# Another order of first loads and first ScalarE work, and dummy products on TensorE, in a graph-attention and expert kernel

## The reference, cut to what matters

```python
def gat_layer(x, adj, W, a_self, a_neigh, b):
    feat = jnp.einsum('nf,hfo->hno', x, W)
    attn_self = jnp.einsum('hno,ho->hn', feat, a_self)
    attn_neigh = jnp.einsum('hno,ho->hn', feat, a_neigh)
    e = jax.nn.leaky_relu(attn_self[:, :, None] + attn_neigh[:, None, :], 0.2)
    e = e + MASK_VAL * (1.0 - adj)[None, :, :]
    alpha = jax.nn.softmax(e, axis=-1)
    out = jnp.einsum('hnm,hmo->hno', alpha, feat) + b[:, None, :]
    return jax.nn.elu(jnp.transpose(out, (1, 0, 2)).reshape(out.shape[1], -1))
x = x + tanh(g_xattn) * gat_twice(ctx_512, layernorm(x))
x = x + tanh(g_ffn) * (routed_experts(layernorm(x)) + shared_experts(layernorm(x)))
```

## Time and profile before

| | us |
|---|---|
| median of three runs | 427.19 |
| the three runs | 427.02, 427.19, 428.5 |
| the profiled execution | 426.62 |
| its span in the trace | 424.9 |

### The profile page before, as it was taken

How to read it: one execution, slowest core, us unless ns; L and a number is a source line. 1 busy time by engine, 2 the same in 40 slices (tenths; PEclk the granted TensorE clock), 3 DMA queues, 4 the chain that set the end, 5 groups by cost and what they waited for, 6 DMA issues and landing times.

```text
span 424.9 us, 7970 instructions
## 1 busy us (share of the span) xinstructions
PE 379.1 (89%) x2706; PEld 327.9 (77%) x2707; DVE 251.3 (59%) x860; ACT 224.1 (53%) x535; POOL 92.5 (22%) x102
## 2 busy tenths in 40 slices
PE   5986776976999699997998999999999999999991
PEld 4754555654788577885887889999999999999980
DVE  1898979889998946876573423334333334344330
ACT  4699799598866618420210237554646454555410
POOL 6642400000000040132207200312121222212121
PEclk9999697599999979999999999999999999999996
DMA  6149387515050001010899920122222222221221
GB/s 177 41 174 427 145 321 313 201 77 200 2 200 2 0 27 52 2 40 13 323 425 424 380 79 26 25 39 40 48 37 42 37 38 37 39 39 26 25 25 13
DMA packets 17138, 48.68 MB, mean 115 GB/s; under 512 B 3232, under 2 KB 13392, under 8 KB 14160
## 3 DMA queue, kind: packets, MB, share of 16 engines
q1 hardware_dynamic: 11200, 40.80, 25.3%
q0 software_dynamic: 4464, 6.26, 8.4%
q10 hardware_dynamic: 1440, 1.18, 0.8%
HBM read 39.46 MB, written 8.77 MB: 114 GB/s over the span
## 4 chain that ended last, share of the span: by engine, by line
PE 67%; DVE 15%; ACT 11%; issue 2%; POOL 1%; DMA 1%; ACTq 0%; POOLq 0%; DVEq 0%
PE ps_c L797 19%; PE ps_o L815 12%; PE ps_c L644 7%; ACT weights L902 6%; PE ps_n L797 5%; PE ps_pt L651 4%; PE ps_n L644 3%; ACT weights L908 3%; DVE weights L1096 3%; PE ps_pt L563 3%; PE ps_f L552 2%; DVE weights L1107 2%; PE ps_n L651 2%; PE ps_o L578 2%; PE ps_n L516 2%
## 5 line engine op out<-in xcount | busy, mean ns | idle before, releaser
L797 PE MATMUL ps_c<-tile_t,weights 128*128 128x128 f32 x736 | 89.6, 275 | 0.0
L797 PEld LDWEIGHTS ps_c<-tile_t,weights 128*128 128x128 f32 x736 | 87.6, 192 | 1.2
L1157 DVE SCALAR_TENSOR_TENSOR gate_silu<-gate_tanh,ps_c 128x256 f32<-128x256 f32 x76 | 31.9, 420 | 78.2 <-ACT gate_tanh L1001 67.3
L476 POOL DMA_INDIRECT out<-y_sb,tile_in x23 | 35.8, 1555 | 145.5 <-DVE y_sb L1337 145.5
L902 ACT ACTIVATE weights<-weights 128x256 f32<-128x256 f32 x128 | 63.1, 498 | 0.6 <-DVE y_sb L1172 0.6
L1096 DVE SCALAR_TENSOR_TENSOR weights<-weights 128x256 f32<-128x256 f32 x128 | 54.4, 487 | 6.2 <-ACT weights L889 5.8
L1006 ACT ACTIVATE weights<-weights 128x2560 f32 x23 | 53.8, 2337 | 6.1 <-issue 6.1
L644 PE MATMUL ps_c<-x_norm_t,weights 128*128 128x256 f32 x240 | 56.6, 383 | 0.0
L563 PE MATMUL ps_pt<-ident,weights 128*128 128x128 f32 x256 | 39.4, 304 | 18.5 <-ACT weights L908 18.5
L815 PE MATMUL ps_o<-weights,hidden 128*128 x230 | 53.5, 380 | 0.6 <-DVE hidden L1160 0.6
L563 PEld LDWEIGHTS ps_pt<-ident,weights 128*128 128x128 f32 x256 | 32.8, 157 | 26.2 <-issue 25.3
(11 more groups left out here) (207 smaller groups left out, 507.7 us busy)
## 6 DMA issues: line engine op xcount, KB each, us to landing
weights<-w_routed SPq DMA_DIRECT2D x8, 1920.0 KB, 21.0
weights<-t_rows SPq DMA_DIRECT2D x14, 1024.0 KB, 5.7
weights<-w_shared SPq DMA_DIRECT2D x1, 3840.0 KB, 16.2
tile_in<-slots SPq DMA_DIRECT2D x23, 132.0 KB, 2.1
slots<-pad_row SPq DMA_DIRECT2D x1, 1188.0 KB, 11.3
out<-y_sb ACTq DMA_DIRECT2D x4, 256.0 KB, 7.2
weights<-x SPq DMA_DIRECT2D x2, 256.0 KB, 3.7
x_in<-x SPq DMA_DIRECT2D x2, 256.0 KB, 4.2
```

Source lines behind the costliest of these rows:

```text
L476: pool.indirect_dma_start(out=out, out_offset=bass.IndirectOffsetOnAxis(ap=tile_in[:, slot, ID_COL:ID_COL + 1].bitcast(U32), axis=0), in_= ...
L797: mm = pe.matmul(ps_chunk[c][:, part * cw + i * P:part * cw + (i + 1) * P], ring[r % RING][:, a:a + P], tile_t[:, r % 2, k, :], start=(k = ...
```

## The change

SyncE's queue loads the context of graph 0 first, and the attention columns `a_cols` move to ScalarE's queue, behind `w0_t`. VectorE clears `x_norm_t[0]` at the start. TensorE multiplies parts of this cleared tile into `ps_c` 8 times ahead of all else, and 3 times at the end of each of the units 0, 1 and 2; nothing reads these products. The mask of graph 0 is made on VectorE. The bends of units 0 and 1 (the first half of the rows of the first graph) read t from PSUM; those of units 2 and 3 read the copy in SBUF. ScalarE makes the 0.2 t copy first and the t copy after the bends that read PSUM. `mask_stats(1)` stands behind `copy_features(1)`, and the tanh of the gates stands in unit 0.

```diff
@@ -56,6 +56,8 @@
 PEELED = 4
 ROUTED_LOOPS = (SLOT_TILES - WEIGHTS_AHEAD - PEELED) // SLOTS_IN
 QUADS = HEADS // QUAD
+WARM_FIRST = 8
+WARM_STEPS, WARM_EACH = 3, 3
 
 
 
@@ -240,7 +242,8 @@
         ring_filled = sem("ring_filled")
         const_step, ident_ready = sem("const_step"), sem("ident_ready")
         ramp_ready = sem("ramp_ready")
-        wide_ready, wide_copied = sem("wide_ready"), sem("wide_copied")
+        wide_ready, wide_copied, wide_scaled = sem("wide_ready"), sem("wide_copied"), sem("wide_scaled")
+        warm_ready, first_masked = sem("warm_ready"), sem("first_masked")
         nodes_ready, t_copied, s_copied = sem("nodes_ready"), sem("t_copied"), sem("s_copied")
         st_t = sem("st_t")
         ld_t = [[sem(f"ld_t{c}{quad}") for quad in range(QUADS)] for c in range(PAIR)]
@@ -312,7 +315,7 @@
             def load_x(n):
                 sp.dma_start(x_in[n], x[n * N:(n + 1) * N, :].rearrange("(h p) d -> p h d", p=P)).then_inc(ld_x[n], 16)
 
-            sp.dma_start(a_sb, a_cols.rearrange("(c p) a -> p c a", p=P)).then_inc(ld_a, 16)
+            load_ctx(0)
             load_x(0)
             load_ctx(1)
             load_x(1)
@@ -445,12 +448,13 @@
                 for half in range(HV):
                     pool.tensor_scalar(mask[n][:, half, :], x_in[n][:, half, :], stats[c][:, half, 6:7], stats[c][:, half, 7:8],
                                        ALU.subtract, ALU.mult).then_inc(mask_step, 1)
-                pool.wait_ge(mask_step, HV * (n + 1))
+                pool.wait_ge(mask_step, HV * n)
                 pool.tensor_scalar(mask[n], mask[n], 1.0, MASK, ALU.subtract, ALU.mult).then_inc(mask_ready, 1)
 
             for n in range(B):
                 power(n, n % PAIR)
-                make_mask(n, n % PAIR)
+                if n > 0:
+                    make_mask(n, n % PAIR)
             for n in range(B):
                 if n == 2:
                     send_rows(0)
@@ -685,6 +689,13 @@
                     pe.wait_ge(hid_ready, PIECES * n + IC * (e + 1))
                     down(n, half, e, ps_n[:, half * D:(half + 1) * D])
 
+            def keep_warm(count):
+
+                for _ in range(count):
+                    pe.matmul(ps_c[:, 0, 0:P], x_norm_t[0][:, 0, 0:P], x_norm_t[0][:, 1, 0:P], start=True, stop=True)
+
+            pe.wait_ge(warm_ready, 1)
+            keep_warm(WARM_FIRST)
             pe.wait_ge(ident_ready, 1)
             pe.wait_ge(ld_a, 16)
             pe.wait_ge(ld_w0_t, 16)
@@ -727,6 +738,8 @@
                     filler(slots_now[1])
                 if u == 3:
                     spread_inverse(L)
+                if w < WARM_STEPS:
+                    keep_warm(WARM_EACH)
                 if w in TURN_X_NORM:
                     pe.wait_ge(h1_read, TURN_X_NORM[w] + 1)
                     turn_x_norm(TURN_X_NORM[w])
@@ -848,10 +861,11 @@
         @block.scalar
         def _(act):
             act.dma_start(w0_t_sb, w0_t.rearrange("(k p) n -> p k n", p=P)).then_inc(ld_w0_t, 16)
-            act.dma_start(ctx_sb[0][0:F_IN, :], ctx_t[0]).then_inc(ld_ctx[0], 16)
-
-            act.wait_ge(ld_gates, 16)
-            act.activation(tanh_gates, gates_sb, ACT.Tanh).then_inc(gates_ready, 1)
+            act.dma_start(a_sb, a_cols.rearrange("(c p) a -> p c a", p=P)).then_inc(ld_a, 16)
+
+            def make_gates():
+                act.wait_ge(ld_gates, 16)
+                act.activation(tanh_gates, gates_sb, ACT.Tanh).then_inc(gates_ready, 1)
 
             def copy_features(L):
                 act.wait_ge(feat_ready, L + 1)
@@ -864,7 +878,8 @@
                 c = n % PAIR
                 act.wait_ge(ld_x[n], 16)
                 if n >= PAIR:
-                    act.wait_ge(mask_ready, n - PAIR + 1)
+                    act.wait_ge(squares_ready, n - 1)
+                    act.wait_ge(*((mask_ready, n - PAIR) if n > PAIR else (first_masked, 1)))
                 for half in range(HV):
                     act.activation(hidden[:, half * D:(half + 1) * D], x_in[n][:, half, :], ACT.Copy,
                                    accum_out=stats[c][:, half, 4:5]).then_inc(moment_step, 1)
@@ -878,9 +893,12 @@
                 ins.then_inc(squares_ready, 1)
 
             def copy_first_wide(quad):
+                act.wait_ge(bent_ready, quad + 1)
+                act.activation(t_wide[0][:, KINDS * quad, :], ps_wide[quad], ACT.Copy).then_inc(wide_copied, 1)
+
+            def scale_first_wide(quad):
                 act.wait_ge(wide_ready, quad + 1)
-                act.activation(t_wide[0][:, KINDS * quad, :], ps_wide[quad], ACT.Copy)
-                act.activation(t_wide[0][:, KINDS * quad + 1, :], ps_wide[quad], ACT.Copy, scale=LEAK).then_inc(wide_copied, 1)
+                act.activation(t_wide[0][:, KINDS * quad + 1, :], ps_wide[quad], ACT.Copy, scale=LEAK).then_inc(wide_scaled, 1)
 
             def copy_nodes(L):
                 act.wait_ge(nodes_ready, L + 1)
@@ -938,14 +956,16 @@
                 act.wait_ge(y_saved, n + 1)
                 act.dma_start(out[n * N:(n + 1) * N, :].rearrange("(h p) d -> p h d", p=P), y_sb).then_inc(st_base, 16)
 
-            mask_stats(1)
+            scale_first_wide(0)
+            copy_nodes(0)
+            scale_first_wide(1)
             copy_first_wide(0)
-            copy_nodes(0)
-            copy_first_wide(1)
             copy_nodes(1)
             copy_features(0)
             exponent(0)
+            copy_first_wide(1)
             copy_features(1)
+            mask_stats(1)
             for w in range(ALL_UNITS):
                 L, u = w // UNITS, w % UNITS
                 slots_now = filler_slots(w)
@@ -965,6 +985,7 @@
                 if w in NODES_AT:
                     copy_nodes(NODES_AT[w])
                 if w == 0:
+                    make_gates()
                     mask_stats(2)
                 if w == UNITS:
                     mask_stats(3)
@@ -1078,6 +1099,16 @@
                 dve.wait_ge(ld_x[0], 16)
                 row_stats(x_in[0], 0, 1)
 
+            def first_mask():
+
+                dve.wait_ge(inv_ready, 1)
+                for half in range(HV):
+                    ins = dve.tensor_scalar(mask[0][:, half, :], x_in[0][:, half, :], stats[0][:, half, 6:7], stats[0][:, half, 7:8],
+                                            ALU.subtract, ALU.mult)
+                link(ins)
+                dve.tensor_scalar(mask[0], mask[0], 1.0, MASK, ALU.subtract, ALU.mult).then_inc(first_masked, 1)
+                dve.wait_ge(first_masked, 1)
+
             def mask_max(w):
 
                 L, u = w // UNITS, w % UNITS
@@ -1088,18 +1119,21 @@
                 if u == 0:
                     dve.wait_ge(s_copied, L + 1)
                 if L == 0:
-                    dve.wait_ge(wide_copied, quad + 1)
+                    dve.wait_ge(wide_scaled, quad + 1)
+                    if half > 0:
+                        dve.wait_ge(wide_copied, quad + 1)
                 else:
                     dve.wait_ge(ld_t[c][quad], 16 * ((L + 1) // PAIR if c else L // PAIR))
+                neigh = ps_wide[quad] if L == 0 and half == 0 else t_wide[c][:, KINDS * quad, :]
                 for i in range(QUAD):
                     h = quad * QUAD + i
                     ins = dve.scalar_tensor_tensor(out=logits[:, w % AHEAD, i * N:(i + 1) * N],
-                                                   in0=t_wide[c][:, KINDS * quad, i * N:(i + 1) * N],
+                                                   in0=neigh[:, i * N:(i + 1) * N],
                                                    scalar=s_cols[c][:, half, h:h + 1],
                                                    in1=t_wide[c][:, KINDS * quad + 1, i * N:(i + 1) * N], op0=ALU.add, op1=ALU.max)
                 ins.then_inc(bent_ready, 1)
-                if u == 0 and layer == 0:
-                    dve.wait_ge(mask_ready, n + 1)
+                if u == 0 and layer == 0 and n > 0:
+                    dve.wait_ge(mask_ready, n)
                 dve.wait_ge(bent_ready, w + 1)
                 for i in range(QUAD):
                     v = logits[:, w % AHEAD, i * N:(i + 1) * N]
@@ -1256,8 +1290,10 @@
             def tail_piece(n, i):
                 shared_piece(n, i, piece_bank(n, i))
 
+            dve.memset(x_norm_t[0], 0.0).then_inc(warm_ready, 1)
             weigh_columns(0)
             first_mask_stats()
+            first_mask()
             mask_max(0)
             mask_max(1)
             weigh_columns(1)
```

## The result

| | kernel before | changed kernel |
|---|---|---|
| median of seven runs | 428.40 us | 431.41 us |
| all runs | 427.02 to 431.32 | 429.61 to 437.17 |
| profiled execution | 426.62 | 432.18 |
| its span | 424.9 | 430.4 |

The ratio is 1.0074, with a 95% interval of 1.004 to 1.0108: slower by 3.2 us, 1.7 to 4.6. More runs of the kernel before have raised its own median from 427.19 to 428.40, so the change cost 3.0 us between medians, where +3.6 was forecast.

A forecast was written before the change was run, and what follows sets the result against it. TensorE until 20.58 us, then ScalarE's chain of exponents, was taken to bound the kernel. 0.85 + 2.27 + 0.15 + 0.3 = +3.6 us on a median of 427.19 gave 430.8 us, range 424.6 to 431.9.

The forecast's parts named there:

- What bounds the start: TensorE's work until 20.58 us bounds the start, then ScalarE's exponents from unit 1 on, which carry the whole kernel.
- The dummies ahead: Eight products before the column sums on TensorE delay the first wide product from 5.10 to 5.95: +0.85 us at low clock.
- The order of loads: At the start, context earlier and columns second on their queue; both wait for TensorE, so nothing is paid back.
- the clock staying low: TensorE stays at its low clock through the start despite the burst; 430.8 us, chance 0.50.
- the rise with a fall: Rival at the start: TensorE's clock rises in the dummies and falls again in 64-row products; 428.1 us, chance 0.25.
- the rise that holds: Rival at the start: TensorE's clock rises and holds to the end of the features; 424.6 us, chance 0.19.
- The statistics: mask_stats(1) on ScalarE, now between the features' copy and the exponents of unit 1, is no longer hidden: +2.27 us.
- The gates: The gates' tanh comes into ScalarE's busy stretch in unit 0: +0.15 us.
- The dummies of the units: TensorE, units 0 to 2: hidden at high clock, 0.75 us stick out at low clock; booked +0.3 us.
- The mask of graph 1: GpSimd ends it at 31.0 us; VectorE waits 3 us for it, covered with 3.5 us to spare.
- Bends from PSUM: VectorE's bends that read PSUM cost the same as those from SBUF, 1.67 us for four.
- That the shift is carried in full: The whole kernel loses what the exponents of unit 1 lose; rival, not carried: about 427 us, chance 0.06.

The follow-up runs named there:

- run 8: Kernel before with only the cleared tile and the 8 dummies ahead added; 1.0010 of the kernel before.
- run 1: Changed kernel without any dummies and without the clearing of the tile; 1.0067 of the kernel before.
- run 12: Changed kernel measured again, unaltered, in six runs; median 428.14 us against 424.66 of the kernel before on the same chip.
- run 2: Changed kernel with the 8 dummies ahead but none in units 0 to 2; 1.0023 of the kernel before.
- run 4: Changed kernel without any dummies and with mask_stats(1) moved back ahead of the first wide copies; 1.0036 of the kernel before.
- run 10: Changed kernel without unit dummies, mask_stats(1) moved back, layer 1 column sums and second features behind unit 0's transposes; 1.0000 of the kernel before.
- run 11: Changed kernel without dummies, old load order, mask_stats(1) moved back, layer 1 column sums and second features behind unit 0's transposes; 1.0002 of the kernel before.
- run 5: Changed kernel without dummies, mask_stats(1) moved back, and the old order of the two first loads; 0.9985 of the kernel before.
- run 9: Kernel before with only the first units reordered, layer 1 column sums and second features behind unit 0's transposes; 0.9987 of the kernel before.
- run 3: Changed kernel, all dummies kept, with mask_stats(1) moved back ahead of the first wide copies; 1.0000 of the kernel before.

## Why the prediction was right, point by point

**What bounds the start.** Right. TensorE's low-clock products bound the start, and ScalarE from the exponents of unit 1 on. In run 8 TensorE ends the features at 19.39 and the exponents of unit 1 start at 19.92; before it was 20.58 and 21.11, the same half microsecond.

**The dummies ahead.** Right in kind, short in size: +0.85 was booked, +1.2 measured. The clearing began at 0.95, not 0.78, and the records took 0.24 us, the dearer of my two rows. The sum as written had a slip too: 4.9 + 0.58 + 0.04 + 0.3 is 5.82, and I wrote 5.95.

**The order of loads.** Missed. I said both loads would wait for TensorE, which holds with the dummies. I gave no price for the columns behind `w0_t`, and without the dummies that is 0.2 to 1.7 us. It also means that in the changed kernel the burst costs less than it seems, because it covers a late load. This is what run 1 stumbled over.

**The clock.** I gave the case that came in the trace, the clock staying low, 0.50, the rise with a fall 0.25, the rise that holds 0.19. Two traces of six with the 8 dummies show the rise and fall, four the low clock; the runs' mean clock speaks for two in three. The rise that holds came in none of the four traces with an early rise: in each the clock fell among the 64-row products, with TensorE busy. That the 64 rows are the cause isn't isolated by any run. The rival's mechanism was right, its chance too low by half, and the reason that I had for the low clock (zeros, of which no row tells) is not one, since zeros raised it in three traces. The plain rule of the Trainium skill, "TensorE: Matmul & The Clock Gate" (Part 1, "What's actually happening"), that activity releases the throttle, agrees with the long bursts (two of two) and with two of six short ones, not with the products from 5.10 to 20.58. My reading of these was too simple in one point: from 16.69 to 18.51 the column sums of layer 1 stand among them, with 128 rows. The Trainium skill's same page (Part 4, "PE-mode transpose") says that transpose-mode work doesn't count as busy for the clock in the same way. Here the clock rose behind eight transposes at 29.36 and the products next to them, so these records at least didn't keep it down; whether they are of the page's mode no row tells.

**The statistics.** Right: 2.27 forecast, 22.28 to 24.54 = 2.26 measured, and moving them back is the largest part of the loss in the times as well (1.0074 to 1.0000 with the dummies, 1.0067 to 1.0036 without; between medians from 3.0 us to 0.3, and from 3.6 to 1.9).

**The gates.** 0.15 forecast, 0.1 measured (24.54 to 29.77 is 5.23, and 21.11 to 26.25 was 5.14).

**The dummies of the units.** A term that the clock decides: +0.3 was booked, and 0.75 for a low clock. In the profiled execution the low clock lasted. The chain that ended last, of the changed kernel (start, us, engine, what), runs through them:

```profile
34.10 1.71 PE ps_pt L567 x8
...
36.82 0.96 PE ps_c L695 x6
...
39.86 0.60 ACT weights L932
```

The transposes of unit 2 stand behind 1.58 us of dummies, and the copy is 0.9 us later for it. From the exponents of unit 1 to the copy of `ps_f` behind unit 3 (L932 at 39.86) ScalarE takes 15.32 us here. It took 14.10 before (21.11 to 35.21). Run 1 has no dummies and as long a low clock: 14.77. Run 12 has all the dummies and the clock up by 31 us: 14.17. So of the 1.22 us more, 0.1 are the gates, some 0.55 the dummies, and the other 0.6 come with the low clock alone, which in the trace of before had ended by the transposes of unit 3 and here lasted through them in run 1 and until about 36.9 us in the changed kernel. The sum had no term for that. Where the clock is up the dummies are hidden, as was forecast.

**The mask of graph 1.** Right: done at 31.2 (31.0 forecast), a wait of 3.05 us (3), covered by ScalarE's lag. **Bends from PSUM.** Right: 1.66 us for four. The page of the Trainium skill that I had weighed, "Perfetto Trace Analysis" ("Optimizing Scalar/DVE Operations"), would have had them longer by 0.26 us, my estimate from its figures; the trace shows no such difference.

**The sum.** For the low clock the exponents of unit 1 were forecast at 24.2 and start at 24.54 in both traces of the changed kernel. At the end 430.8 was forecast and 431.41 measured, and that is closer than the sum deserves. The kernel before's own median moved up by 1.2 us, and the change cost 3.0 and not 3.6. Up to the copy behind unit 3 the profiled execution lost 4.65 us, 1.05 more than the sum (0.35 in the burst, the rest in the units), and about two executions in three seem to get some 2 us back by a clock that I had at one in four. These errors cancel.

**That the shift is carried in full.** I named as a sign of being wrong that the shift isn't that of the end, and between the two single traces it isn't: 4.65 us at the copy of `ps_f` behind unit 3, nothing at 175 us, 5.5 at the end. Over all the kernels it is carried, though not to the microsecond. The table has that copy in each trace against the 35.21 of before, and the difference of the medians:

| kernel | copy at, us | against before | medians | ratio |
|---|---|---|---|---|
| changed | 39.86 | +4.65 | +3.0 | 1.0074 |
| run 12, changed again | 38.71 | +3.5 | +3.5 | none |
| run 2 | 38.70 | +3.5 | +3.0 | 1.0023 |
| run 1 | 38.34 | +3.1 | +3.6 | 1.0067 |
| run 4 | 36.49 | +1.3 | +1.9 | 1.0036 |
| run 10 | 36.21 | +1.0 | +0.8 | 1.0000 |
| run 11 | 36.15 | +0.9 | +0.9 | 1.0002 |
| run 5 | 34.92 | -0.3 | -1.0 | 0.9985 |
| run 8, clock rose | 34.21 | -1.0 | +0.6 | 1.0010 |
| run 9 | 33.98 | -1.2 | -1.15 | 0.9987 |
| run 3, clock rose | 33.78 | -1.4 | +0.3 | 1.0000 |

The rows that are off by more than 1 us are the changed kernel and runs 3 and 8, each with a burst, whose trace shows one of the two ways that the clock can go while the median mixes both. So a shift at 36 us is worth about as much at the end, as the prediction took it; that it is worth exactly as much the intervals of 0.3 to 0.4% can't tell.

## What to carry to other kernels

Work that lies in an idle stretch of the engine that becomes the chain a few microseconds later is free only there: find the chain's engine for each stretch before you move anything on it. Dummy products are not a price-free warm-up: count them at the low clock against the first data, and expect the lift in some executions only; here it was lost again within the first 3 us of 64-row products. Where a change is worth less than 1%, read the first stage trace by trace, but trust the end only over a dozen runs of both kernels. And before a gain or a loss late in one trace is put down to the change, see whether a second trace has it: the 3.5 us that seemed to be given back here were a bad stretch in the one trace of before.

## What the runs showed of the hardware

- Products with 64 rows did not raise TensorE's clock in 15.5 us without a gap (trace of before, with 1.8 us of 128-row column sums among them), and did not hold it: in four traces it fell some 2.5 us after the first of them (an estimate from 3.31 to 3.54 us for the second wide product instead of 1.96). No run changes the rows alone.
- Zeros raise the clock as ones do: from 0.24 to 0.11 us a record, near 5.5 and 5.6 us, for a burst that began at 1.5. A burst of 3.8 us raised it in two traces of six, one of 7.5 us in two of two.
- The attention columns (32 KB in pieces of 64 bytes), put second on a queue, landed at 4.26 us in one execution and 5.27 in another; first on the other queue they were never what the column sums waited for, which began at 3.34 to 3.45.
- The profile shows the clock as full until its first change, so that a low clock at the start is seen only in the durations.
